# Cross attention in a two-layer decoder: latent queries by pairs of batches, as three fp32r products of 512 columns

## Chip, cores, metric

One core of a Trainium2 chip runs the whole kernel. The metric is the device time of one execution in microseconds, the median of several runs. Engines: TensorE (PE; its weight loads are shown as PEld), VectorE (DVE), ScalarE (ACT), GpSimd (POOL), and SyncE (SP), which issues the DMA transfers.

## What is computed

A decoder with two layers over x of shape (4, 256, 256) and a context of (4, 256, 64). Layer 0 is linear attention with decay, an additive cross term and a mixture of experts; layer 1 is softmax attention with rotary embedding, a cross attention with latents (the part that is changed), and another mixture of experts. A layer norm stands ahead of each part, whose output is added to x. The cross attention has 16 heads, a query latent of 192, a context latent of 64:

```python
DIM_Q, H, K, D_C, D_CQ, R = (256, 16, 128, 64, 192, 64)
# Wq (H*K, DIM_Q), w_kc_q (H, K, D_CQ), w_kc_kv (H, K, D_C)
# W_qr (H, D_CQ, R), W_kr (H, D_C, R), Wo (DIM_Q, H*K)
def _rotate_half(x):
    half = x.shape[-1] // 2
    return jnp.concatenate([-x[..., half:], x[..., :half]], axis=-1)
def _apply_rope(x, sin, cos):
    return x * cos + _rotate_half(x) * sin
```

As the kernel does it: the queries x Wq are taken into the query latent by w_kc_q, rotated, and taken by W_qr and W_kr to the 64 features of the context latent, where they meet the rotated context. Softmax over 256 context positions, the weighted context, and then w_kc_kv and Wo give the output.

## The kernel before

The program is written by hand, one instruction stream for each engine, with semaphores between them. Cross attention (`cross()` in each engine's stream) has a merging stage and a loop.

**Merging stage.** Weights arrive in four groups of four heads (`wx`, two buffers of 2 MB; the third and fourth wait until the first and second have been used). For each group TensorE computes merged queries (`merged_queries`, L1854: Wq times w_kc_q, one PSUM bank a head, banks 0 to 3), merged keys (L1867: W_qr times W_kr, banks 4 and 5) and merged outputs (L1878: w_kc_kv times Wo, bank 6). ScalarE copies the queries (L1237) and the outputs (L1230); VectorE writes the keys with a head mask in twelve 128x64 pieces a group (L836) into `merged_s`, which GpSimd has zeroed (L1330). Each group also transposes the tokens of one batch into bank 7 (L1915), and ScalarE copies them to `xT4` (L1242). After the second group TensorE computes the latent queries of the first unit, while the weights of the third are on their way. VectorE rotates the keys (L841, L843), and TensorE then transposes them (L1927).

**Loop.** There are 16 units, w = 4 batch + group, one batch of 256 tokens and one group of four heads each (L2005). A group's query latent is three tiles of 128 rows, each with two halves (`part`) for the rotation. `latent_queries(w, j)` (L1890) is one tile: two parts by two K halves, f32 128x128 by 128x256, into bank n % 2. The profile shows each f32 product as two records, so a tile is 8 records. VectorE multiplies by cosine and sine (`rope`, L820 and L821, 128x512 each), GpSimd adds the two halves into `latent_rot` (L1337, two additions of 128x256 a tile). `query_side(w)` (L1930) multiplies by `merged_s` into bank 2; ScalarE rounds the result to fp32r (`tSh`, L1266), VectorE computes the rest (`tSl`, L849), and both are wanted by `scores` (L1946, fp32r, split in three products). VectorE takes maxima (L856), ScalarE exponentials (L1252), VectorE scales (L866), TensorE transposes (L1978), ScalarE and VectorE copy (L1258, L871). `weighted_contexts` (L1982) and `output` (L1991) follow. The outputs of a batch's four units are accumulated in bank 7 and added to x once a batch (L876).

The order within a unit is written out by hand (L2005 to L2029). Latent queries of unit w+1 stand between the steps of unit w: after its query side, between the two blocks of transposes of unit w-1, and after its second scores. The output is that of unit w-2. After the loop, the expert stage of layer 1 begins, interleaved with the last unit. Its weights go through `raw` (SyncE loads, ring of five), `whi` (ScalarE) and `wlo` (VectorE): high part and rest, in fp32r, three products each (`three`, L1762).

## Time and profile before

| | us |
|---|---|
| median of 3 runs | 911.11 |
| lowest, highest | 910.43, 911.59 |
| the profiled execution | 910.82 |
| its span in the profile | 909.0 |
| TensorE busy | 887.6 (98%) |
| VectorE busy | 615.3 (68%) |
| ScalarE busy | 424.0 (47%) |
| GpSimd busy | 101.3 (11%) |

The profiled execution took 910.82 us, 1.8 more than the span of its instructions. The merging stage begins with merged queries at 414.27 us from the span's start; the loop starts at 441.13, and its last unit's scores at 672.65. TensorE's granted clock is at its full level (0.997 on average). Matmuls are pipelined, and a record lasts longer than the distance to the next one: the distance between starts is what a record costs.

### The profile page before, as it was taken

How to read it: one execution, taken by the hardware profiler on the slowest of the kernel's cores; microseconds unless marked ns; L12 is line 12 of the kernel's file. 1: busy time of each engine (PE TensorE's matmuls, PEld its weight loads, DVE VectorE, ACT ScalarE, POOL GpSimd, SP SyncE). 2: the span in 40 equal slices, each digit the busy share in tenths (PEclk: the TensorE clock that was granted, in tenths of full speed). 3: DMA queues.
4: the chain of work that ended last, by engine and by line, in shares of the span. 5: the costliest groups of instructions: out<-in, count | busy, mean ns of one | idle time of the engine just before them, and what ended most of it. 6: DMA issues, size and time to landing. Idle time of an engine off the chain costs nothing.

```text
span 909.0 us, 14200 instructions
## 1 busy us (share of the span) xinstructions
PE 887.6 (98%) x5377; PEld 687.1 (76%) x5377; DVE 615.3 (68%) x1185; ACT 424.0 (47%) x1063; POOL 101.3 (11%) x128
## 2 busy tenths in 40 slices
PE   8998999999999999999999999999999999999998
PEld 5665778888888876667877777777767778888886
DVE  4679656666666667657787786877785566666665
ACT  8554643343443479863543444344354444333342
POOL 4011000000000220003122232322210000000000
PEclk9999999999999999999999999999999999999999
DMA  6003111111100500006200000000010111111001
GB/s 189 1 7 119 36 52 53 39 48 52 35 0 1 231 1 2 1 1 265 91 2 1 1 1 1 1 1 2 0 36 18 36 53 52 53 35 52 17 0 47
DMA packets 12537, 37.10 MB, mean 41 GB/s; under 512 B 2080, under 2 KB 4352, under 8 KB 11712
## 3 DMA queue, kind: packets, MB, share of 16 engines
q1 hardware_dynamic: 12448, 36.32, 12.0%
q8 instruction: 37, 0.61, 0.3%
q14 instruction: 20, 0.16, 0.1%
q0 software_dynamic: 32, 0.01, 0.0%
HBM read 35.27 MB, written 1.05 MB: 40 GB/s over the span
## 4 chain that ended last, share of the span: by engine, by line
PE 85%; DVE 7%; ACT 5%; DMA 1%; issue 1%; POOL 0%; DVEq 0%; ACTq 0%
PE ps L1345 79%; PE ps L1978 3%; PE ps L1518 2%; DMA wx<-in_wx 1%; DVE P L542 1%; ACT Q L1134 1%; DVE stats L466 1%; ACT DT L950 1%; DVE xn L474 0%; ACT probs_q L1252 0%; ACT whi L1149 0%; DVE weighted_h L694 0%; DVE probs_q L866 0%; PE ps L1356 0%; DVE wlo L810 0%
## 5 line engine op out<-in xcount | busy, mean ns | idle before, releaser
L1179 ACT ACTIVATE h_hi<-weighted_h 128x512 fp32r<-128x512 f32 x100 | 63.2, 632 | 150.9 <-DVE weighted_h L694 148.8
L704 DVE TENSOR_TENSOR h_lo<-weighted_h,h_hi 128x512 fp32r<-128x512 f32 x100 | 69.2, 692 | 66.1 <-ACT h_hi L1179 65.9
L1345 PE MATMUL ps<-xT_first,whi 128*128 128x512 f32 x376 | 109.0, 391 | 1.2 <-ACT silu_g L1174 1.2
L1345 PE MATMUL ps<-xT_second,whi 128*128 128x512 f32 x376 | 108.5, 391 | 1.3 <-ACT silu_g L1174 1.2
L731 DVE TENSOR_TENSOR shared_gate<-silu_g,row_shares 128x512 f32<-128x512 f32 x88 | 60.9, 692 | 61.2 <-ACT silu_g L1174 61.0
L1174 ACT ACTIVATE silu_g<-ps 128x512 f32<-128x512 f32 x100 | 59.7, 598 | 73.4 <-PE ps L1345 73.4
L1345 PE MATMUL ps<-xT,merged_q 128*128 128x256 f32 x384 | 91.9, 383 | 0.0
L1337 POOL TENSOR_TENSOR latent_rot<-rope_buf 128x256 f32<-128x256 f32 x96 | 68.4, 733 | 180.4 <-DVE rope_buf L821 180.4
L1345 PEld LDWEIGHTS ps<-xT_first,whi 128*128 128x128 f32 x376 | 70.3, 188 | 17.3 <-issue 2.8
L1345 PEld LDWEIGHTS ps<-xT_second,whi 128*128 128x128 f32 x376 | 70.1, 188 | 17.0 <-issue 2.5
L1345 PEld LDWEIGHTS ps<-xT,merged_q 128*128 128x128 f32 x384 | 70.4, 190 | 10.5
L1345 PE MATMUL ps<-h_hi,wlo 128*128 128x512 f32 x200 | 78.0, 390 | 0.0
L1345 PE MATMUL ps<-h_hi,whi 128*128 128x512 f32 x188 | 74.2, 395 | 0.8 <-DVE h_lo L704 0.7
L1345 PE MATMUL ps<-h_lo,whi 128*128 128x512 f32 x188 | 73.3, 390 | 0.0
L1252 ACT ACTIVATE probs_q<-ps,neg_max 128x256 f32<-128x256 f32 x128 | 58.9, 472 | 28.7 <-DVE neg_max L856 28.7
L694 DVE TENSOR_TENSOR weighted_h<-ps,shared_gate 128x512 f32<-128x512 f32 x88 | 60.9, 692 | 8.4
L1345 PE MATMUL ps<-xT_second,wlo 128*128 128x512 f32 x200 | 61.7, 390 | 0.0
L1345 PE MATMUL ps<-xT_first,wlo 128*128 128x512 f32 x200 | 61.7, 390 | 0.0
L1134 ACT ACTIVATE Q<-ps,nm 128x256 f32<-128x256 f32 (+1 forms) x128 | 52.5, 449 | 2.4 <-DVE nm L551 2.4
L866 DVE TENSOR_SCALAR probs_q<-probs_q,rsum 128x256 f32<-128x256 f32 x128 | 49.9, 451 | 1.1
L1345 PE MATMUL ps<-latent_rot,merged_s 128*64 128x256 f32 (+1 forms) x256 | 47.4, 386 | 0.0
L1345 PEld LDWEIGHTS ps<-latent_rot,merged_s 128*64 128x64 f32 (+1 forms) x256 | 32.0, 163 | 19.3 <-issue 14.5
(197 smaller groups left out, 1572.7 us busy)
## 6 DMA issues: line engine op xcount, KB each, us to landing
raw<-in_ffn SPq DMA_DIRECT2D x50, 384.0 KB, 3.0
wx<-in_wx SPq DMA_DIRECT2D x4, 2048.0 KB, 11.2
cx<-in_cx SPq DMA_DIRECT2D x1, 1536.0 KB, 8.2
X<-in_x SPq DMA_DIRECT2D x4, 256.0 KB, 6.8
kvc<-in_kvc SPq DMA_DIRECT2D x1, 1024.0 KB, 14.3
out<-X SPq DMA_DIRECT2D x4, 256.0 KB, 2.2
wqkv<-in_wqkv SPq DMA_DIRECT2D x1, 768.0 KB, 8.2
wqkv<-in_wqkv SPq DMA_DIRECT2D x1, 512.0 KB, 6.3
```

What stands on the lines that cost most here:

```text
L694: v.tensor_tensor(weighted_h[:, u % 2, :], ps[:, 5 + u % 2, :], gate[:, u % 2, :], ALU.mult).then_inc(weighted[l], 1)
L704: v.tensor_tensor(h_lo[:, u % 2, :], weighted_h[:, u % 2, :], h_hi[:, u % 2, :].bitcast(F32), ALU.subtract).then_inc(act_lo[l], 1)
L731: v.tensor_tensor(shared_gate[:, u % 2, :], silu_g[:, u % 2, :], row_shares[:, hf, :], ALU.mult).then_inc(gated[l], 1)
L866: last = v.tensor_scalar(probs_q[:, w % 2, st, ab, pair, :], probs_q[:, w % 2, st, ab, pair, :], rsum[:, st, ab, pair:pair + 1], None, ALU ...
L1134: last = a.activation(Q[:, n % 3, i, width * h:width * h + width], step_scores(n)[:, i, width * h:width * h + width], ACT.Exp, bias=nm[:, ...
L1174: a.activation(silu_g[:, u % 2, :], ps[:, gate_bank(n), :], ACT.Silu).then_inc(silu_done[l], 1)
L1179: a.activation(h_hi[:, u % 2, :], weighted_h[:, u % 2, :], ACT.Copy).then_inc(act_hi[l], 1)
L1252: last = a.activation(probs_q[:, w % 2, st, ab, pair, :], ps[:, xscore_bank(ab), 256 * pair:256 * pair + 256], ACT.Exp, bias=neg_max[:, st ...
L1337: g.tensor_tensor(latent_rot[:, TILE_ORDER[j], part, :], r1[:, j, 256 * part:256 * part + 256], r2[:, j, 256 - 256 * part:512 - 256 * part ...
L1345: return pe.matmul(o, l, r, start=start, stop=stop, skip_group_check=True)
L1518: last = pe.transpose(ps[:, bank, 128 * c:128 * c + 128], src, ident)
L1978: last = pe.transpose(ps[:, turned_bank(ab), 256 * pair + 128 * st:256 * pair + 128 * st + 128], probs_q[:, w % 2, st, ab, pair, 128 * lt: ...
```

## The change

1. Units go by pairs of batches: w counts batch of the pair fastest, then group, then pair. A pair is what one set of latent queries serves, 512 tokens at once.
2. A latent query chunk is one tile and one part, for two batches (`latent_chunk`): 48 chunks, each three products (high weights by high tokens, low weights by high tokens, high weights by low tokens) by two K halves, in fp32r with 512 columns. So merged query weights and tokens are both split: ScalarE writes the high part, VectorE subtracts it from PSUM for the low part (`merged_ql`, second half of `xT_first` and `xT_second`). PSUM banks of the merging stage are free only after VectorE (`merged_q_low`, `xt_rest`).
3. Chunks run two units ahead instead of one: six in the merging stage (three after the second group, three after the third), three in each of the units 0 to 13, none in 14 and 15.
4. GpSimd adds pairs of chunks (128x512). The middle tile's result has two buffers. GpSimd, not VectorE, now rotates the keys, and it zeroes nothing.
5. Merged keys: one masked VectorE operation a part; the middle tile's two heads are swapped in the layout, so that a piece less is stored.
6. Each unit's output is added to x by itself (128x512), no longer accumulated over four units; batches 0 and 1 are normalised in units 10 and 11, batches 2 and 3 after the loop.
7. The expert weights of layer 1 have other places (`raw1`, `whi1`) and are loaded after the last chunk; ScalarE's first three splits of them stand in units 14 and 15.

```diff
-    for name, width in (("wq", 4 * D), ("kcq", 4 * XQ), ("qrT", 2 * 4 * LO), ("krT", 4 * XC), ("kckv", 4 * XC), ("woT", 4 * D)):
+    for name, width in (("wq", 4 * D), ("kcq", 4 * XQ), ("qrT", 2 * 4 * LO), ("krT", 6 * XC), ("kckv", 4 * XC), ("woT", 4 * D)):
...
+        def unit_batch(w):
+
+            return 2 * (w // (2 * GROUPS)) + w % 2
+
+        def unit_group(w):
+
+            return w // 2 % GROUPS
+
+        def latent_chunk(n):
+
+            pair, c = divmod(n, 6)
+            return pair, TILE_ORDER[c // 2], c % 2
...
+                if l == 1:
+                    sp.wait_ge(pe_latent, LATENT_CHUNKS)
...
+                def rope(n):
+
+                    pair, tile, part = latent_chunk(n)
                     v.wait_ge(pe_latent, n + 1)
-                    if w >= 1:
-                        v.wait_ge(latent_rotated, 2 * (n - 3) + 2)
...
+                    if n >= 3:
+                        v.wait_ge(latent_rotated, 2 * ((n - 3) // 2 + 1))
...
+                for hg in range(GROUPS):
+                    if hg % 2 == 0:
+                        merged_key_parts(hg)
+                    for jj in range(4):
+                        v.wait_ge(merged_q_copied, 4 * hg + jj + 1)
+                        v.tensor_tensor(merged_ql[:, hg, :, :, LO * jj:LO * jj + LO], ps[:, jj, 0:2 * XQ].rearrange("p (k h f) -> p k h f", k=KD, h=2),
+                                        merged_qh[:, hg, :, :, LO * jj:LO * jj + LO].bitcast(F32), ALU.subtract).then_inc(merged_q_low, 1)
+                    if hg % 2:
+                        merged_key_parts(hg)
+                    v.wait_ge(xt_ready, 8 + hg + 1)
+                    tokens, at = (xT_first, xT_second)[hg // 2], 256 * (hg % 2)
+                    v.tensor_tensor(tokens[:, 1, :, at:at + 256], ps[:, 7, :].rearrange("p (k s) -> p k s", k=KD), tokens[:, 0, :, at:at + 256].bitcast(F32),
+                                    ALU.subtract).then_inc(xt_rest, 1)
+                    if hg == 1:
+                        v.wait_ge(cx_in, 16)
+                    if hg in (1, 2):
+                        for j in range(CHUNKS_PER_UNIT):
+                            rope(CHUNKS_PER_UNIT * (hg - 1) + j)
...
+                def add_output(w):
+                    b, last = unit_batch(w), unit_group(w) == GROUPS - 1
+                    v.wait_ge(pe_xout, w + 1)
...
+            for i in range(LATENT_CHUNKS // 2):
+                pair, tile, _ = latent_chunk(2 * i)
+                g.wait_ge(rope_products, 4 * i + 4)
+                if tile == 1 and pair >= 2:
+                    g.wait_ge(pe_operand, 2 * pair - 2)
+                elif tile != 1 and pair >= 1:
+                    g.wait_ge(pe_operand, 2 * pair)
+                for part in range(2):
+                    g.tensor_tensor(rotated(pair, tile)[:, part, :], r1[:, (2 * i + part) % 3, :], r2[:, (2 * i + 1 - part) % 3, :], ALU.add).then_inc(latent_rotated, 1)
...
                     if hg >= 1:
-                        pe.wait_ge(merged_q_copied, 4 * (hg - 1) + jj + 1)
+                        pe.wait_ge(merged_q_low, 4 * (hg - 1) + jj + 1)
                     if hg == 2 and jj < 2:
                         pe.wait_ge(rope_products, 6 - 2 * jj)
+                    if hg == 3 and jj < 2:
+                        pe.wait_ge(rope_products, 10 + 2 * jj)
...
+                    for m, (weights, token_part) in enumerate(((merged_qh, 0), (merged_ql, 0), (merged_qh, 1))):
                         for kk in range(KD):
-                            last = mm(ps[:, n % 2, 256 * part:256 * part + 256], merged_q[:, hg, kk, part, 128 * tile:128 * tile + 128], xT4[:, kk, b, :], kk == 0, kk == 1)
+                            last = mm(ps[:, n % 2, :], weights[:, hg, kk, part, 128 * tile:128 * tile + 128], tokens[:, token_part, kk, :], m + kk == 0, m + kk == 3)
...
+                    if hg in (1, 2):
+
+                        pe.wait_ge(xt_rest, 2)
+                        pe.wait_ge(merged_q_low, 4 * hg + 2)
+                        for j in range(CHUNKS_PER_UNIT):
+                            latent_queries(CHUNKS_PER_UNIT * (hg - 1) + j)
+
+                pe.wait_ge(merged_q_low, 4 * GROUPS)
+                pe.wait_ge(xt_rest, NB)
                 pe.wait_ge(kv_rotated, 1)
...
                 for w in range(UNITS):
-                    more = w + 1 < UNITS
-                    if w == 1:
-                        latent_queries(2, 0)
+                    ahead = CHUNKS_PER_UNIT * (w + 2)
+                    more = ahead < LATENT_CHUNKS
                     query_side(w)
-                    if more and w != 1:
-                        latent_queries(w + 1, 0)
-                    if not more:
+                    if more:
+                        latent_queries(ahead)
+                    else:
                         output(w - 2)
                     scores(w, 0)
```

## Rows read from the trace of the kernel before

**Rows 1.** The page: busy time; TensorE's group of latent queries

```profile
PE 887.6 (98%) x5377; PEld 687.1 (76%) x5377; DVE 615.3 (68%) x1185; ACT 424.0 (47%) x1063; POOL 101.3 (11%) x128
L1345 PE MATMUL ps<-xT,merged_q 128*128 128x256 f32 x384 | 91.9, 383 | 0.0
```

**Rows 2.** Timeline of TensorE in a steady unit: start, length, what, count, [idle]

```profile
537.78 0.39 PE L1345 MATMUL ps<-kvh,tSh 64*128 64x256 f32 x2
...
538.69 1.99 PE L1345 MATMUL ps<-xT,merged_q 128*128 128x256 f32 x8
540.52 1.89 PE L1345 MATMUL ps<-merged_o,wqkv 128*128 128x256 f32 x8
...
544.10 2.96 PE L1345 MATMUL ps<-latent_rot,merged_s 128*64 128x256 f32 x16
546.90 1.89 PE L1345 MATMUL ps<-xT,merged_q 128*128 128x256 f32 x8
548.72 0.39 PE L1345 MATMUL ps<-kvh,tSh 64*128 64x256 f32 x2
```

**Rows 3.** The same timeline: first scores of units 13, 14 and 15

```profile
641.56 0.39 PE L1345 MATMUL ps<-kvh,tSh 64*128 64x256 f32 x2
...
657.17 0.38 PE L1345 MATMUL ps<-kvh,tSh 64*128 64x256 f32 x2
...
672.65 0.39 PE L1345 MATMUL ps<-kvh,tSh 64*128 64x256 f32 x2
```

**Rows 4.** The same timeline in the expert stage of layer 0

```profile
201.28 0.39 PE L1345 MATMUL ps<-h_hi,whi 128*128 128x512 f32 x1
...
202.41 0.39 PE L1345 MATMUL ps<-h_lo,whi 128*128 128x512 f32 x1
```

**Rows 5.** Timelines of ScalarE, VectorE, TensorE between query side and scores

```profile
547.10 0.60 ACT L1266 ACTIVATE tSh<-ps 128x512 fp32r<-128x512 f32 x1 [2.18 <-PE ps L1345]
...
547.73 0.69 DVE L849 TENSOR_TENSOR tSl<-ps,tSh 128x512 fp32r<-128x512 f32 x1 [2.32 <-ACT tSh L1266]
...
456.86 0.69 DVE L849 TENSOR_TENSOR tSl<-ps,tSh 128x512 fp32r<-128x512 f32 x1 [1.16 <-ACT tSh L1266]
...
457.60 0.39 PE L1345 MATMUL ps<-kvh,tSh 64*128 64x256 f32 x2 [1.41 <-DVE tSl L849]
```

**Rows 6.** Timeline of TensorE: second scores of unit 15

```profile
676.73 0.39 PE L1345 MATMUL ps<-kvh,tSh 64*128 64x256 f32 x2 [0.46 <-ACT probs_q L1252]
```

**Rows 7.** Groups of GpSimd (busy, mean ns); timelines of VectorE and GpSimd

```profile
L1337 POOL TENSOR_TENSOR latent_rot<-rope_buf 128x256 f32<-128x256 f32 x96 | 68.4, 733 | 180.4 <-DVE rope_buf L821 180.4
L1327 POOL TENSOR_TENSOR P<-P 128x512 f32<-128x512 f32 x8 | 10.2, 1273 | 230.1 <-DVE P L490 230.1
...
540.21 1.14 DVE L866 TENSOR_SCALAR probs_q<-probs_q,rsum 128x256 f32<-128x256 f32 x4
...
542.67 2.09 DVE L866 TENSOR_SCALAR probs_q<-probs_q,rsum 128x256 f32<-128x256 f32 x4
...
542.63 1.46 POOL L1337 TENSOR_TENSOR latent_rot<-rope_buf 128x256 f32<-128x256 f32 x2 [2.83 <-DVE rope_buf L821]
```

**Rows 8.** The chain that ended last; merging stage: TensorE's timeline, ScalarE's copies (min/median/max)

```profile
646.02 0.60 DVE rope_buf L821
...
417.07 11.86 DMA wx<-in_wx
...
417.72 5.38 PE L1345 MATMUL ps<-wx 128*128 128x192 f32 x36 [0.24 <-ACT merged_q L1237]
...
423.53 5.34 PE L1345 MATMUL ps<-xT,merged_q 128*128 128x256 f32 x24
...
428.97 5.41 PE L1345 MATMUL ps<-wx 64*128 64x128 f32 x36
...
441.13 3.01 PE L1345 MATMUL ps<-latent_rot,merged_s 128*64 128x256 f32 x16
...
L1237 ACT ACTIVATE merged_q<-ps x16: 482/491/548, 417.1 to 437.5; 128x384 f32<-128x384 f32 x16
```

More of the change, by code:

```diff
@@ L347, in build, with rotated, output_added @@
         UNITS = NB * GROUPS
+        CHUNKS_PER_UNIT = 3
+        LATENT_CHUNKS = CHUNKS_PER_UNIT * UNITS
         TILE_ORDER = (1, 0, 2)
+        def unit_batch(w):
[5 more added lines that the diff above has]
+            return pair, TILE_ORDER[c // 2], c % 2
+        def rotated(pair, tile):
+            return middle_rot[:, pair % 2] if tile == 1 else outer_rot[:, tile // 2]
+        def output_added(w):
+            if unit_group(w) < GROUPS - 1:
+                return x_added, (2 * GROUPS - 2) * (w // (2 * GROUPS)) + w % (2 * GROUPS) + 1
+            return x_done, 8 * 4 + 2 * unit_batch(w) + 2
         def xscore_bank(ab):
@@ L881, in cross @@
                 for w in range(UNITS):
-                    more = w + 1 < UNITS
+                    ahead = CHUNKS_PER_UNIT * (w + 2)
+                    more = ahead < LATENT_CHUNKS
                     operand_rest(w)
+                    if not more and w >= 2:
+                        add_output(w - 2)
                     if more:
-                        rope(w + 1, 0)
-                    else:
+                        rope(ahead)
+                    elif w == UNITS - 1:
                         split_lo(1, 0, 0)
@@ L891, in cross @@
                     if more:
-                        rope(w + 1, 1)
-                    else:
+                        rope(ahead + 1)
+                    elif w == UNITS - 1:
                         split_lo(1, 1, 1)
@@ L896, in cross @@
                         copy_transposed(w - 1, 1)
-                    if w == 0:
-                        rope(1, 2)
                     row_max(w, 1)
                     normalise_probs(w, 0)
-                    if more and w >= 1:
-                        rope(w + 1, 2)
+                    if more:
+                        rope(ahead + 2)
                     normalise_probs(w, 1)
-                    if w % GROUPS == 1 and w > 1:
-                        add_output(w // GROUPS - 1)
-                    if w % GROUPS == 2 and w > 2:
-                        normalise(5, w // GROUPS - 1)
+                    if more and w >= 2:
+                        add_output(w - 2)
+                    if w in (2 * GROUPS + 2, 2 * GROUPS + 3):
+                        normalise(5, w - 2 * GROUPS - 2)
                 tokens_low(1, 0)
+                add_output(UNITS - 2)
                 copy_transposed(UNITS - 1, 0)
@@ L1930, in query_side @@
                 def query_side(w):
-                    pe.wait_ge(latent_rotated, 6 * w + 2)
+                    pair_of_batches, columns = w // 2, slice(256 * (w % 2), 256 * (w % 2) + 256)
+                    pe.wait_ge(latent_rotated, 6 * pair_of_batches + 2)
                     if w >= 1:
                         pe.wait_ge(operand_lo, w)
-                    group = w % GROUPS
+                    group = unit_group(w)
                     for part in range(2):
@@ L1938, in query_side @@
                             half = slice(64 * (1 - pair), 64 * (1 - pair) + 64)
-                            mm(ps[half, 2, 256 * pair:256 * pair + 256], merged_s[:, group, part, 1 + pair, half], latent_rot[:, 1, part, :], part == 0, False)
+                            mm(ps[half, 2, 256 * pair:256 * pair + 256], merged_s[:, group, part, 1, half], rotated(pair_of_batches, 1)[:, part, columns], part == 0, False)
                     for pair in range(2):
-                        pe.wait_ge(latent_rotated, 6 * w + 4 + 2 * pair)
+                        pe.wait_ge(latent_rotated, 6 * pair_of_batches + 4 + 2 * pair)
                         for part in range(2):
-                            last = mm(ps[:, 2, 256 * pair:256 * pair + 256], merged_s[:, group, part, 3 * pair, :], latent_rot[:, 2 * pair, part, :], False, part == 1)
+                            last = mm(ps[:, 2, 256 * pair:256 * pair + 256], merged_s[:, group, part, 2 * pair, :], rotated(pair_of_batches, 2 * pair)[:, part, columns], False, part == 1)
                     last.then_inc(pe_operand, 1)
                 def scores(w, st):
-                    b = w // GROUPS
+                    b = unit_batch(w)
                     if w == 0 and st == 0:
@@ L2017, in cross @@
                     if more:
-                        latent_queries(w + 1, 1)
+                        latent_queries(ahead + 1)
                     if w >= 1:
                         transposed_probabilities(w - 1, 1)
-                    if w == 0:
-                        latent_queries(1, 2)
                     scores(w, 1)
-                    if more and w >= 1:
-                        latent_queries(w + 1, 2)
+                    if more:
+                        latent_queries(ahead + 2)
                     if w >= 2 and more:
@@ L2070, in constants @@
     head = (np.arange(3)[None] * P + p[:, None]) // LO
-    put("gmask", head[:, :, None] == np.arange(3)[None, :, None] + np.arange(2)[None, None, :])
+    put("gmask", head[:, :, None] == np.array(TILE_HEADS)[None])
     put("even", (p // HD) % 2 == 0)
@@ L2125, in cross_pack @@
     put("qrT", by_group(i["L1_xattn_W_qr"].reshape(XH, 2, LO, XR), 0, 4, 2, 1, 3))
-    put("krT", by_group(i["L1_xattn_W_kr"], 0, 3, 1, 2))
+    put("krT", by_group(i["L1_xattn_W_kr"], 0, 3, 1, 2)[:, :, [h for pair in TILE_HEADS for h in pair]])
     put("kckv", by_group(i["L1_xattn_w_kc_kv"], 0, 2, 1, 3))
```

176 lines of the change are left out of this document (84 added, 92 removed).

## The prediction

> **What bounds the kernel now.** I read the page first: TensorE is busy for 98% of the span, and its largest group inside cross attention is the latent queries, 384 records of 128x256 f32 [rows 1]. Then one unit of cross attention (of 16) in TensorE's timeline. Call S0 and S1 the two score blocks of a unit, L a block of latent queries, T transposed probabilities, O the output, W weighted contexts, Q the query side of the next unit. The order is S0, T, L, T, S1, L, O, W, Q, L. S0 starts at 548.72 and at 641.56: six units, 15.47 us each, with no idle bracket on TensorE [rows 2, 3]. So in the steady units anything that leaves TensorE's queue is worth its time, until the chain through ScalarE, VectorE and GpSimd that feeds it is late. So the question of the whole reading is where those chains end.
>
> **Records of latent queries.** An L of 8 f32 records takes 1.82 us (546.90 to 548.72) [rows 2], 0.2275 a record. An fp32r product with 512 columns is one record; five in a row in the expert stage start 0.226 apart (201.28 to 202.41) [rows 4]. A record thus costs the same and only the count matters. Before: 48 blocks x 8 = 384. After: 48 chunks x 6 = 288 (three products x two K halves, for two batches at once). Removed: 96 x 0.2275 = 21.8 us of TensorE work. A chunk takes 6 x 0.227 = 1.36 us in place of 1.82.
>
> **Steady units (2 to 12).** Taking three times 0.455 out of 15.47 leaves 14.10. Three chains could be late.
> (a) Between Q and S0: ScalarE rounds the operand 0.20 after L starts (547.10 against 546.90), VectorE's rest starts 0.63 later (547.73) [rows 2, 5]. Where it is exposed, the rest runs from 456.86, 0.69 long, and S0 starts at 457.60 [rows 5]. So S0 cannot start sooner than 0.20+0.63+0.69+0.05 = 1.57 after L. L used to cover this with 1.82; at 1.36 it no longer does: 0.21 of stall per unit.
> (b) S0 to S1 waits for four exponentials. In the last unit, where nothing covers them, it is 676.73-672.65 = 4.08, ended by ScalarE [rows 3, 6]. In a steady unit it is 15.47-(548.72-537.78) = 4.53 [rows 2], and 0.455 less is 4.08: just covered.
> (c) Rotation by GpSimd. It now adds pairs of chunks, 128x512 each; such an addition takes 1.27, a 128x256 one 0.73 [rows 7]. So it works in bursts of 2.55 us, and in odd units the last burst begins after the third rotation product. VectorE's work from S0 is: two products (0.6 each [rows 8]) to 1.15, two maxima to 2.4, a copy to 3.0, two products to 4.5 (waiting for L), copy to 5.1, maxima to 6.4, scaling to 7.6, products to 8.85. The burst ends at 11.45. S1 lasts 0.91 and O and W 3.58 together (540.52 to 544.10), so Q starts at 4.08+0.91+1.36+3.58 = 9.95 and reaches the products that need it after two thirds of its 2.80 us [rows 2], at 11.8. Margin 0.35 us, so no stall, but little room.
> The new addition of each unit's output (128x512, 0.6 on VectorE, in place of two smaller ones every fourth unit) falls at 11 to 12.6, before the operand rest at 13.6, hidden; without that cover it would be 0.6 a unit. O waits only for the addition of a unit earlier.
> A steady unit is 14.10+0.21 = 14.31, a gain of 1.16; eleven of them: **-12.8 us**. Bounds: 14.10 (chain (a) shorter than it looks) to 14.9 (0.3 at (b), 0.6 at (c) in every other unit), -15 to -6.
>
> A row bears on (c): scaling four 128x256 tiles takes 1.14 alone, but 2.09 when it starts at 542.67 beside a GpSimd burst that starts at 542.63 [rows 7]. Bursts now last 2.55, so VectorE could lose about 1.9 there in an odd unit rather than 0.95; that ends at 12.0, still before 13.6, and is not in the sum. The Trainium skill (SBUF — State Buffer, "Who interferes with whom") says that the two engines lock a shared port pair for a whole instruction and that the loser fully blocks. By that rule the longer instructions block VectorE longer, which speaks against this change. The trace agrees as to the direction (2.09 against 1.14), and by either reading the loss lies in VectorE's slack.
>
> **Merging stage: what is added.** All of the first pair's chunks (6, not 3 blocks) now stand here: 6x1.36 - 5.34 [rows 8] (at 423.53) = +2.8 us of work. The rest is new waiting, since a PSUM bank comes free only after VectorE has subtracted, behind ScalarE's copy (0.49) [rows 8]. VectorE's 128x384 subtraction is not in this trace; 0.46 is scaled from 0.60 for 512, bounds 0.2 and 0.6. Step by step:
> - The second group's merged queries start at 417.72 now [rows 8]. VectorE first has the merged keys (2 x 0.46 where twelve small ones stood) and then four subtractions from 418.4, first done 418.9: **1.2** late. The whole group then ends at 424.5 with its transposes.
> - The first chunk needs the second batch's tokens too: merged-output copy, token copy, subtraction (0.5+0.5+0.6): it starts at 426.0, not 423.53, **1.5** of it idle.
> - Three chunks end at 430.15. The weights that ended the wait at 428.93 [rows 8] are 3% larger and should have landed; that wait goes, and what is late next is TensorE itself.
> - Third group and transposes, 5.6: chunks 3 to 5 run 435.75 to 439.95. The rotation of chunk 5 reuses a buffer of chunk 2, which GpSimd reads from 438.55 (after chunk 3's products) to 441.1. Its products end at 442.4, and the fourth group's second head waits for that bank: **1.8** idle. GpSimd itself has the rotation of the keys first (three 1024-wide operations, an estimate of 2.4 each at twice 1.27, from 424 to 431.2); the first pair is rotated by 433.8, in time.
> - Fourth group to 447.3; then the last tokens' copy and subtraction (**1.4**), key transposes, and the loop starts at 449.4 instead of 441.13.
> Sum: **+8.3 us**. Bounds: +2.8 if no new wait shows, +10 if subtractions take 0.6 and each hand-over 0.1 more.
>
> **First and last units.** From loop start to the second unit's S0: 457.60-441.13 = 16.47 now [rows 5, 8]. After: Q 2.80, 1.57, S0 to S1 3.9 (no copy ahead of the exponentials), 0.91, 1.36, 2.80, 1.57 = 14.91: **-1.6**. Unit 1 has no O, so Q starts at 8.2 and its last products would be due at 10.05, before the GpSimd burst ends at 11.45: 13.95 against 641.56-11x15.473-457.60 = 13.76: **+0.2**. Unit 13: two L go, the last L becomes an O of the same length, 657.17-641.56 = 15.61 less 0.91, plus small change: **-1.05**. Unit 14 has no latent queries left, so it is bound by the exponentials as unit 15 is: 4.08, S1 0.91, W 1.76, Q 2.80 and O 1.82 = 11.4 against 672.65-657.17 = 15.48 [rows 3]: **-4.1**. At the end, an addition (0.6 [rows 8]), statistics (an estimate of 0.7, two reads of 256 columns) and the normalisation of the third batch move into the tail beside other work; in unit 15 two additions come before its maxima: **+0.4** (bounds 0 and 2).
>
> Moved transfers: the expert weights' first five loads wait for the last chunk, near 640, and are needed near 658; such a load lay well under that apart, so nothing. Both queues' other work keeps its place.
>
> **Sum.** +8.3-1.6+0.2-12.8-1.05-4.1+0.4 = -10.65. The profiled execution took 910.82 (span 909.0, 1.8 around it): 900.2 after, with a span of 898.4. The median of the runs is 0.3 above the profiled one: 900.5.
>
> **Rivals.**
> 1. *New waits don't bite.* If the merging stage costs only its +2.8 of work plus some 1.5, and (a) is covered, the sum is +4.3-1.6-15.1-1.05-4.1+0.4 = -17: about 894. For: VectorE has slack in that stage; against: the ring TensorE, ScalarE, VectorE is traced step by step above. 15%.
> 2. *The GpSimd burst is late in odd units.* Margin is 0.35. If the third rotation products slip by 1 us (blocked scaling, other order), six odd units lose 0.65, (b) loses 0.2 in eleven: +6, about 906.5. 15%.
> 3. *Slower: changing between f32 and fp32r.* At a change of type the first record may cost more. If entry and exit each cost 0.2 us, 48 chunks lose 19 us, and the result is about 920. It decides from 10.6/48 = 0.22 a chunk. Against it: the score blocks are fp32r between f32 blocks already and no gap stands at 548.72 [rows 2]. 4%.
> 4. *Gains and costs cancel:* waits of rival 2 in every unit and the upper bound in the merging stage, near 911. 3%.
>
> **How the numbers follow.** The forecast, 897 to 904 around 900.5, has 63%, the rivals 15, 15, 4 and 3. The range 892.5 to 908 takes in rivals 1 and 2 and leaves out 3 and 4 and the ends of the bounds. 0.2% (1.8 us) is about what a measurement here can tell from no change. Faster 0.93, same 0.03, slower 0.04.
>
> **What the profile after would show.** 288 latent-query records of 128x512, 0.227 apart; S0 14.3 us apart in the steady units, with a 0.2 idle bracket before it released by VectorE's operand rest; some 35 us from the first group to the loop start with idle brackets before the second group, the first chunk, the fourth group's second head and the key transposes; an S0 distance of 11.4 in unit 14. The prediction is wrong if the loop starts before 446 or after 452, if TensorE waits for GpSimd in odd units, or if a chunk takes over 1.5 us.

## The result, and the profile after

| | us |
|---|---|
| after, median of 5 runs | 906.5 (905.9 to 907.8) |
| before, median of 5 runs beside it | 910.89 |
| ratio after/before, 95% interval | 0.9954 (0.9942 to 0.9965) |
| the profiled execution after, and its span | 906.39, 904.6 |

The change is faster by 4.4 us, beyond the 0.2% that can be told from no change; the forecast was a gain of 10.65. The page of after: TensorE is busy for 13.6 us less than in [rows 1], but the span is only 4.4 shorter, so some 9 us of idle time were added. GpSimd has fewer instructions (79 for 128) and is busy for 3 us less.

```profile
PE 874.0 (97%) x5281; PEld 666.8 (74%) x5281; DVE 628.5 (69%) x1170; ACT 421.4 (47%) x1063; POOL 98.1 (11%) x79
```

The gain does not lie where the time was added, so the first thing to make is a ledger by stage, from the starts in TensorE's timeline of either kernel:

| stage | before | after | moved | forecast |
|---|---|---|---|---|
| start to the first merged queries | 414.27 | 414.51 | +0.24 | 0 |
| merging stage, to the loop's start | 26.86 | 36.98 | +10.12 | +8.3 |
| loop's start to S0 of unit 1 | 16.47 | 15.26 | -1.21 | -1.6 |
| unit 1 | 13.75 | 14.23 | +0.48 | +0.2 |
| units 2 to 12 | 170.21 | 160.11 | -10.10 | -12.8 |
| unit 13 | 15.61 | 14.98 | -0.63 | -1.05 |
| unit 14 | 15.48 | 11.35 | -4.13 | -4.1 |
| S0 of unit 15 to the end | 236.35 | 237.18 | +0.83 | +0.4 |
| sum | | | -4.40 | -10.65 |

Two terms carry most of the miss of 6.25: the steady units (2.7) and the merging stage (1.8). The other six add 1.7.

**A steady unit after.** TensorE's timeline from S1 of one unit to S0 of the next (start, length, what, count, [idle]):

```profile
484.22 1.03 PE L2043 MATMUL ps<-cst,probs_q 128*128 128x128 f32 x8
485.18 0.39 PE L1405 MATMUL ps<-kvh,tSh 64*128 64x256 f32 x2
...
486.09 0.73 PE L1405 MATMUL ps<-xT_first,merged_qh 128*128 128x512 f32 x2
...
487.57 1.89 PE L1405 MATMUL ps<-merged_o,wqkv 128*128 128x256 f32 x8
...
491.16 1.03 PE L1405 MATMUL ps<-middle_rot,merged_s 128*64 128x256 f32 x8
...
493.77 0.82 PE L1405 MATMUL ps<-xT_first,merged_qh 128*128 128x512 f32 x2
...
495.53 0.39 PE L1405 MATMUL ps<-kvh,tSh 64*128 64x256 f32 x2
```

The chunk behind S1 lasts 487.57-486.09 = 1.48. The block that it replaces lasted 540.52-538.69 = 1.83 [rows 2], so 0.35 is saved and not the 0.455 of the forecast. Transposes and the block behind them went from 2.65 to 2.33, 0.32 less.

The block behind Q has to be read together with Q. From Q's start to S0 it was 548.72-544.10 = 4.62 and is 495.53-491.16 = 4.37, exactly the forecast's 2.80+1.57. Q looks 0.19 shorter (2.61 for 2.80) and the chunk behind it 0.19 longer than forecast (1.76 for 1.57), but that is one thing counted twice: the chunk's first record starts earlier beside Q's last ones. ScalarE, which needs the finished Q, starts 2.99 behind Q's start, 3.00 before. The whole unit: 0.32+0.35+0.25 = 0.92, and the period went from 15.47 to 14.55.

Does chain (a) hold S0 up? TensorE's timeline shows no idle bracket, because a matmul record ends later than the next one may start. The lines of ScalarE and VectorE, and the chunk's last record:

```profile
494.15 0.60 ACT L1317 ACTIVATE tSh<-ps 128x512 fp32r<-128x512 f32 x1 [2.18 <-PE ps L1405]
494.79 0.69 DVE L894 TENSOR_TENSOR tSl<-ps,tSh 128x512 fp32r<-128x512 f32 x1 [2.44 <-ACT tSh L1317]
495.12 0.39 PE L1405 MATMUL ps<-xT_first,merged_qh 128*128 128x512 f32 x1
```

S0 starts at 495.53, 0.05 behind the end of the operand rest (494.79+0.69), as where it was exposed before (457.60, [rows 5]). So chain (a) does end last. Its size: S0 stands 0.41 behind the chunk's last record. Before, where the operand rest ended 0.30 ahead of S0 (548.72 against 547.73+0.69), that distance was 0.31 (548.72-548.41). So the wait is 0.10 a unit, not the 0.21 of the forecast; the longer chunk fills the rest. The weight loads say about the same:

```profile
495.53 0.19 PEld L1405 LDWEIGHTS ps<-kvh,tSh 64*128 64x128 f32 x2 [0.46 <-DVE tSl L894]
548.72 0.19 PEld L1345 LDWEIGHTS ps<-kvh,tSh 64*128 64x128 f32 x2 [0.33 <-DVE tSl L849]
```

The first line is after's and the second before's. A bracket of 0.33 that names VectorE stands there even where nothing is late, so only the 0.13 above it count.

**Why 0.35 and not 0.455.** Three answers of TensorE's timeline of before, with windows that begin inside a block, give its single records; under them, after's records of one chunk:

```profile
538.69 0.48 PE L1345 MATMUL ps<-xT,merged_q 128*128 128x256 f32 x1
539.01 0.59 PE L1345 MATMUL ps<-xT,merged_q 128*128 128x256 f32 x2
539.22 1.46 PE L1345 MATMUL ps<-xT,merged_q 128*128 128x256 f32 x6
```

```profile
486.43 0.39 PE L1405 MATMUL ps<-xT_first,merged_qh 128*128 128x512 f32 x1
```

Before, the second record starts 0.32 after the first (539.01-538.69) and the other starts are (540.52-539.01)/7 = 0.216 apart. After, the second starts 0.34 after the first (486.43-486.09) and the others are (487.57-486.43)/5 = 0.229 apart. So the f32 record of 256 columns is cheaper than the fp32r record of 512, and a block has some 0.1 beside its records: behind the scores at its entry (as here), ahead of the scores at its exit (the 0.31 above). Before's block between two blocks of transposes has none of it, 552.28-550.55 = 1.73 for eight records:

```profile
550.55 1.89 PE L1345 MATMUL ps<-xT,merged_q 128*128 128x256 f32 x8
552.28 1.04 PE L1978 MATMUL ps<-cst,probs_q 128*128 128x128 f32 x8
```

The prediction divided the 1.82 of the block ahead of the scores by 8, which spread that 0.1 over the records and gave 0.2275. Eight records at 0.216 less six at 0.229 to 0.232 are 0.33 to 0.35, and 48 chunks save about 16.6 us, not 21.8.

**The merging stage after.** TensorE's timeline, with the brackets to look for:

```profile
414.51 2.76 PE L1405 MATMUL ps<-wx 128*128 128x192 f32 x16
...
419.25 5.38 PE L1405 MATMUL ps<-wx 128*128 128x192 f32 x36 [1.55 <-DVE merged_ql L876]
...
426.63 0.74 PE L1405 MATMUL ps<-xT_first,merged_qh 128*128 128x512 f32 x2 [1.41 <-DVE xT_first L882]
...
444.10 4.73 PE L1405 MATMUL ps<-wx 128*128 128x192 f32 x32 [1.76 <-DVE rope_buf L861]
...
450.88 0.68 PE L1991 MATMUL ps<-cst,wqkv 64*128 64x64 f32 x8 [1.46 <-issue]
451.49 1.08 PE L1405 MATMUL ps<-middle_rot,merged_s 128*64 128x256 f32 x8
```

The four waits stand where the forecast had put them (1.2, 1.5, 1.8, 1.4) and measure 1.55, 1.41, 1.76 and 1.46. The last one's bracket names no releaser; VectorE's subtraction of the last tokens ends at 450.78, 0.10 ahead of the key transposes, as the forecast had it.

### The profile page after: what moved, and what is told of

The parts are those of the page before. It is cut to its first block, busy times and chain, and to the rows that moved or that the text cites. A ratio compares the mean times of both kernels' runs of the same rounds, so it can differ in the third digit from the quotient of the medians.

```text
span 904.6 us, 13933 instructions
## 1 busy us (share of the span) xinstructions
PE 874.0 (97%) x5281; PEld 666.8 (74%) x5281; DVE 628.5 (69%) x1170; ACT 421.4 (47%) x1063; POOL 98.1 (11%) x79
## 3 DMA queue, kind: packets, MB, share of 16 engines
HBM read 35.54 MB, written 1.05 MB: 40 GB/s over the span
## 4 chain that ended last, share of the span: by engine, by line
PE 82%; DVE 9%; ACT 6%; issue 2%; POOL 1%; DVEq 0%; ACTq 0%; POOLq 0%
PE ps L1405 76%; PE ps L2043 3%; PE ps L1578 2%; DVE P L580 1%; ACT Q L1184 1%; ACT probs_q L1303 1%; POOL outer_rot L1398 1%; DVE stats L504 1%; DVE rope_buf L861 1%; DVE xn L512 1%; ACT DT L1000 1%; ACT whi L1199 0%; DVE wlo L848 0%; DVE weighted_h L732 0%; DVE neg_max L901 0%
## 5 line engine op out<-in xcount | busy, mean ns | idle before, releaser
L861 DVE TENSOR_TENSOR rope_buf<-ps,cx 128x512 f32<-128x512 f32 x96 | 61.7, 684 | 9.4 <-PE ps L1405 6.9
L911 DVE TENSOR_SCALAR probs_q<-probs_q,rsum 128x256 f32<-128x256 f32 x128 | 54.5, 488 | 1.1
L1398 POOL TENSOR_TENSOR outer_rot<-rope_buf 128x512 f32<-128x512 f32 x32 | 41.4, 1313 | 100.4 <-DVE rope_buf L861 100.4
L589 DVE TENSOR_REDUCE nm<-ps 128x4 f32<-128x1024 f32 (+1 forms) x24 | 29.2, 1219 | 24.6 <-PE ps L1405 24.6
L848 DVE TENSOR_TENSOR wlo<-raw,whi 128x768 fp32r<-128x768 f32 x47 | 45.0, 957 | 1.9
L1405 PEld LDWEIGHTS ps<-xT_second,wlo 128*128 128x128 f32 x200 | 37.5, 188 | 8.0
## 6 DMA issues: line engine op xcount, KB each, us to landing
kvc<-in_kvc SPq DMA_DIRECT2D x1, 1024.0 KB, 14.6
```

The source lines that it names most:

```text
L848: v.tensor_tensor(wlo[:, slot, :], (raw0, raw1)[l][:, slot, :], high_weights(l, c // RING if isinstance(c, int) else c, slot)[:, slot, :]. ...
L861: v.tensor_tensor(r[:, n % 3, :].rearrange("p (b s) -> p b s", b=2), x, kx(table)[:, at:at + 256].unsqueeze(1).to_broadcast([P, 2, SEQ]), ...
L911: last = v.tensor_scalar(probs_q[:, w % 2, st, ab, pair, :], probs_q[:, w % 2, st, ab, pair, :], rsum[:, st, ab, pair:pair + 1], None, ALU ...
L1398: g.tensor_tensor(rotated(pair, tile)[:, part, :], r1[:, (2 * i + part) % 3, :], r2[:, (2 * i + 1 - part) % 3, :], ALU.add).then_inc(laten ...
L1405: return pe.matmul(o, l, r, start=start, stop=stop, skip_group_check=True)
```

## The experiments

All comparisons are with the kernel before, run beside them on the same chip (910.45 in the first group, 910.74 and 910.7 in the others); after is 906.5, measured beside 910.89.

**1. Four products in place of three** (`e2_four_products`): eight records a chunk.

```diff
-  for m, (weights, token_part) in enumerate(((merged_qh, 0), (merged_ql, 0), (merged_qh, 1))):
+  for m, (weights, token_part) in enumerate(((merged_qh, 0), (merged_ql, 0), (merged_qh, 1), (merged_ql, 1))):
```

> Changed kernel with a fourth product in each chunk (low weights by low tokens), 8 records for 6. Theory A: blocks two and three of a unit cost 0.45 more each, the one after the query side 0.25 (its own 1.56 grows to 2.01, where 1.76 is spent now), 1.16 x 14 = 16, and up to 2.7 in the merging stage: 922 to 925. Rival B: 96 x 0.227 = 21.8 more, about 928.3. Theory A above all expects that taking two records away (the other run) gives half of what adding two costs; B expects the same of both.

Measured: 926.18 (925.29 to 927.23), ratio 1.017 (1.0153 to 1.0187). S0 goes from 486.22 to 502.07 without an idle bracket, a period of 15.85, 1.30 above after's 14.55. The chunks behind T and S1 grew by 0.46 to 0.47 for two records and the one behind Q by 0.38, because it had 0.1 of wait in it. So a record costs 0.23 on the path, and the 0.1 beside the records is not paid again. The time is 1.2 above the first theory's range and 2.1 below the rival's. The period grew by 0.14 more than expected (11 units, 1.5 us), and the clock, too, took a part: behind the wait ahead of the key transposes the granted clock is 0.50 from 454 to 456, and the eight records of `outer_rot` take 3.32 where after's take 1.99.

```profile
452.30 0.68 PE L1991 MATMUL ps<-cst,wqkv 64*128 64x64 f32 x8 [1.46 <-issue]
...
454.23 3.32 PE L1405 MATMUL ps<-outer_rot,merged_s 128*128 128x256 f32 x8
```

**2. Two products in place of three** (`e1_two_products`): the product of the high weights with the low tokens is left out, and with it one of the two correction terms.

```diff
-  for m, (weights, token_part) in enumerate(((merged_qh, 0), (merged_ql, 0), (merged_qh, 1))):
+  for m, (weights, token_part) in enumerate(((merged_qh, 0), (merged_ql, 0))):
```

> Changed kernel with one of the three products of each latent-query chunk left out (high weights by low tokens), so 4 records a chunk for 6; its output lacks that term. Theory A (a block costs an entry of about 0.11 us and 0.227 a record; the block between query side and scores is covered by the chain ScalarE to VectorE, and the block between the first and second scores by the exponentials): the first block gives nothing, the second 0.12, the third 0.45 a unit, 0.57 x 14 = 8, and some 1.5 in the merging stage: about 897. Rival B (TensorE's records are all on the path): 96 x 0.227 = 21.8 less, about 884.7.

Measured: 902.09 (901.15 to 902.38), ratio 0.9906 (0.9889 to 0.9922). Both numbers are missed, the first theory's by 5. Its steady unit nearly holds (14.05 on average over units 2 to 12, 13.98 expected), and the timeline shows why taking away records is worth so little there, waits ahead of S0 and of S1:

```profile
552.27 0.39 PE L1405 MATMUL ps<-kvh,tSh 64*128 64x256 f32 x2 [0.48 <-DVE tSl L894]
556.34 0.39 PE L1405 MATMUL ps<-kvh,tSh 64*128 64x256 f32 x2 [0.27 <-ACT probs_q L1303]
566.36 0.39 PE L1405 MATMUL ps<-kvh,tSh 64*128 64x256 f32 x2 [0.48 <-DVE tSl L894]
```

But the merging stage lasts 451.74-414.20 = 37.54, where after's lasts 36.98 and its shorter chunks should have made it shorter. The busy time by stretches (length; busy time of PE, PEld, DVE, ACT, POOL with counts; granted clock, DMA share, GB/s) shows it in the column of the clock:

```profile
442.00:444.00 2.00, 1.33 (x5) 1.36 (x6) 0.99 (x2) 0.00 (x0) 1.40 (x2) 0.71 0.03 8
444.00:446.00 2.00, 2.00 (x8) 2.00 (x7) 0.61 (x2) 0.98 (x2) 1.16 (x1) 0.50 0.00 0
...
452.00:454.00 2.00, 2.00 (x12) 1.34 (x9) 1.67 (x2) 0.00 (x0) 0.00 (x0) 0.77 0.00 0
454.00:456.00 2.00, 2.00 (x7) 1.57 (x5) 0.00 (x0) 0.00 (x0) 0.00 (x0) 0.50 0.00 0
```

Twice the granted clock falls to 0.50, the lower of its two levels (1.2 GHz), for some 3 us. TensorE's timeline of the same stretch has what stood before it and what was slow behind it:

```profile
442.67 6.41 PE L1405 MATMUL ps<-wx 128*128 128x192 f32 x32 [1.95 <-DVE rope_buf L861]
...
451.13 0.68 PE L1991 MATMUL ps<-cst,wqkv 64*128 64x64 f32 x8 [1.46 <-issue]
...
452.75 3.48 PE L1405 MATMUL ps<-outer_rot,merged_s 128*128 128x256 f32 x8
```

TensorE had been idle for 1.95 and for 1.46. The 32 records of merged queries last 6.41 where after's last 4.73, and the eight of `outer_rot` 3.48 where after's last 1.99. That is 1.7 in the merging stage and 1.5 in the loop's first Q, 3.2 us together and most of the 5 by which the first theory missed. Without the 1.7 the stage would be 1.1 shorter than after's, not by the 2.7 of its twelve records fewer: in each half the third chunk now waits for its bank (0.52 and 0.73, VectorE's rotation). After had idle stretches of 1.76 and 1.46 at the same places and kept its clock at 1.00.

**3. f32 products of 512 columns** (`e3_f32_chunks`): the pairing and all the rest of the change, but one f32 product of the rounded high parts in place of the three fp32r ones (both low parts are left out of the product, though still computed).

```diff
-  for m, (weights, token_part) in enumerate(((merged_qh, 0), (merged_ql, 0), (merged_qh, 1))):
-      for kk in range(KD):
-          last = mm(ps[:, n % 2, :], weights[:, hg, kk, part, 128 * tile:128 * tile + 128], tokens[:, token_part, kk, :], m + kk == 0, m + kk == 3)
+  for kk in range(KD):
+      last = mm(ps[:, n % 2, :], merged_qh[:, hg, kk, part, 128 * tile:128 * tile + 128].bitcast(F32), tokens[:, 0, kk, :].bitcast(F32), kk == 0, kk == 1)
```

> Changed kernel with each chunk as f32 products of 512 columns (two, one a K half) in place of six in fp32r; the operands are the rounded high parts and the low parts are left out, though VectorE still writes them. It separates the pairing of batches from the split. If an f32 record costs by its columns (0.2157 at 256, so 0.43 at 512), a chunk is 0.11 + 4 x 0.43 = 1.83 against 1.47: 0.36 more in two blocks of a unit and 0.1 in the covered one, 0.82 x 14 = 11.5, and about 2 in the merging stage: about 920, so pairing alone costs 9 against the kernel before, and the split brings 13.5. Rival: the pairing itself (fewer, longer instructions, fewer entries) brings part of the gain, and the time stays under 911.

Measured: 919.11 (918.87 to 919.24), ratio 1.0094 (1.0077 to 1.0111), as expected. This splits the change: pairing, splitting and the new merging stage cost 8.7 us by themselves, and fp32r products in place of f32 ones give back 12.6.

**4. Output between query side and scores** (`e4_output_after_query`). From unit 2, O takes the place of the chunk between Q and S0, and the unit's three chunks stand between the scores: Q, O, S0, T, L, L, T, L, S1, W.

```diff
                     query_side(w)
-                    if more:
+                    if w < 2:
                         latent_queries(ahead)
                     else:
                         output(w - 2)
                     scores(w, 0)
...
+                    if w >= 2 and more:
+                        latent_queries(ahead)
                     if more:
                         latent_queries(ahead + 1)
```

> Changed kernel, from the third unit on the output of unit w-2 stands between the query side and the scores in place of a latent chunk, and the three chunks stand between the two scores. Theory A: the 1.57 us of ScalarE and VectorE are covered by the output's 1.82, nothing waits, and a unit is 14.34 for 14.55: 12 x 0.21 = 2.5 less, 904. Rival: the wait isn't what the block costs, and it only moves (to GpSimd's additions before an even unit's query side, or to VectorE): 906.5 or more.

Measured: 904.21 (903.64 to 905.78), ratio 0.9936 (0.992 to 0.9953), as expected. The period falls from 14.55 to 14.28, with one unit of 14.9 (609.85 to 624.77). The bracket of the loads ahead of S0 falls from 0.46 to between 0.33 and 0.35, the size that it has where nothing waits: O, 1.82 long, covers chain (a), which the chunk did not. But the wait was only 0.10 to 0.13, so less than half of the 0.27 comes from it, and the number agrees partly by luck. The order also has fewer changes of block; TensorE's timeline shows a block of 12 records in one piece:

```profile
540.14 0.72 PE L1407 MATMUL ps<-xT_second,merged_qh 128*128 128x512 f32 x2
...
543.02 1.03 PE L2045 MATMUL ps<-cst,probs_q 128*128 128x128 f32 x8
```

12 records in 2.88, where two blocks of six take 1.49+1.48 = 2.97: one entry less, 0.09 saved. What is left of the 0.27, some 0.05 to 0.08, is not taken apart.

**5. The merging stage's order** (`e5_last_group`, `e6_all_groups`). In the fourth group the token transposes go first, then keys and outputs, then the queries, and of these the heads whose banks wait for the rotation (0 and 1) go last (`head_order` gives 3, 2, 0, 1). In the second kernel the first two groups are treated alike: tokens ahead of keys and outputs, and VectorE subtracts low queries and low tokens ahead of the key parts.

```diff
-                for jj in range(4):
+                for jj in head_order(hg):
...
+                    if hg == 3:
+                        turned_batch(hg)
-                    if hg == 2:
+                    if hg >= 2:
                         merged_keys(hg)
                         merged_outputs(hg)
                     merged_queries(hg)
```

> From the changed kernel, the order within the fourth group of the merging stage: its token transposes stand first, then the merged keys and outputs, then the four heads' queries with the two outer heads last swapped to the front (3, 2, 0, 1). The key transposes wait for one low part fewer. The arithmetic is the same. Theory A (the stage lost more than forecast by waits of its order: 1.76 before the fourth group's second head and 1.46 before the key transposes in the changed kernel's trace): both waits go, the loop starts 3 to 3.8 us earlier, nothing else changes: 903. Theory B (the stage is paced by its inputs, the weights' DMA and GpSimd's rotation, and the waits only move): the loop starts within 0.5 us of 451.5, 906 or more.

> The fourth group as in the run before, and in groups 0 to 2 the token transposes first too, with VectorE subtracting the low tokens and low queries ahead of the key parts in groups 0 and 1. Theory A: the waits of 1.55 and 1.41 at the start of the stage of the changed kernel shrink as well, which gives 0.5 to 2 us more: 901 to 902.5. Theory B (the early waits are waits for the weights' transfer, which the order does not touch): the same time as the run before within 0.5 us.

Measured: 903.61 (902.98 to 904.7), ratio 0.9921 (0.9905 to 0.9938), and 901.02 (900.22 to 901.41), ratio 0.989 (0.9874 to 0.9907). Both as the first theory had it. The merging stage lasts 449.10-415.62 = 33.48 in the first and 446.30-415.12 = 31.18 in the second, where after's lasts 36.98. In both runs the stage began later than in after, by 1.1 and 0.6, ahead of anything that was changed, and so the time fell by less than the stage. TensorE's timeline of the second:

```profile
419.22 2.84 PE L1421 MATMUL ps<-wx 128*128 128x192 f32 x16 [0.91 <-DVE merged_ql L888]
421.90 0.60 PE L1987 MATMUL ps<-cst,xn 128*128 128x128 f32 x4
422.43 2.62 PE L1421 MATMUL ps<-wx 64*128 64x128 f32 x20
424.97 0.73 PE L1421 MATMUL ps<-xT_first,merged_qh 128*128 128x512 f32 x2
...
439.79 0.60 PE L1987 MATMUL ps<-cst,xn 128*128 128x128 f32 x4
440.32 5.41 PE L1421 MATMUL ps<-wx 64*128 64x128 f32 x36
445.67 0.71 PE L2014 MATMUL ps<-cst,wqkv 64*128 64x64 f32 x8
446.30 1.08 PE L1421 MATMUL ps<-middle_rot,merged_s 128*64 128x256 f32 x8
```

Three of the four waits are gone and the first is 0.91. They came from the order of the steps, not from the weights' transfer.

**6. Both** (`e7_groups_and_output`): the reordered merging stage and O between Q and S0.

> The run before with the output block between the latent query block and the scores from unit 2 on. Theory A (the two gains lie in different stretches and add up; the loop's order alone gave 906.4 to 904.2): 898.5 to 900. Theory B (an earlier loop start meets the same data later, or the stage's gain is given back at the loop's start): 902 or more.

Measured: 897.78 (897.29 to 898.05), ratio 0.9856 (0.9839 to 0.9872). The gains add up, and a little more: 5.5 and 2.3 alone, 8.7 together. This is the fastest kernel that computes everything, 13 us below before, three times what the change itself gave.

**7. Two products again, on that order** (`e8_two_products_reordered`); the edit of experiment 2 on the kernel of experiment 6, with the same term left out.

> The last kernel (merging stage reordered, output between query side and scores) with the product by the low tokens left out: four records a chunk in place of six (the latent queries' smallest term is missing). Alone, on the changed kernel's order, this cut gave 4.3 us of the 21.8 that 96 records take; its trace showed waits on both sides of the scores and TensorE's granted clock at half (0.50) for some 2 us at 444 and 2 at 454, behind idle stretches of the merging stage. Theory A (what stood in the way there is the order: the operand's and the exponentials' chains were exposed, and the idle stretches that preceded the low clock are gone in this order): a steady unit falls from 14.28 by nearly 6 x 0.227 = 1.36 to 12.9-13.1, the merging stage loses 1.5 to 2.7, no stretch at half clock in 440 to 460: 880 to 886. Theory B (VectorE, GpSimd and ScalarE bound a unit whatever the order): the period stays above 13.7, and it ends at 891 to 895.

Measured: 886.58 (886.18 to 890.77), ratio 0.9747 (0.9721 to 0.9773), 11.2 below the kernel of experiment 6, where the same cut on after's order gave 4.4. The granted clock stays at 1.00 from 412 to 462, as the first theory had it. The merging stage itself gives only 1.0 (30.18 for 31.19) and not the 1.5 to 2.7 expected: each half's third chunk waits for its bank (0.52 and 0.74), and the third group for its weights:

```profile
429.15 5.41 PE L1423 MATMUL ps<-wx 64*128 64x128 f32 x36 [0.47 <-DMA wx<-in_wx]
```

Most of the gain comes from the loop (units 2 to 12: 147.7 for 157.6). S1 goes from 506.57 to 519.45 (12.88, as the first theory had it) and then to 533.21 (13.76). The time is 0.6 above that theory's range; the short gain of the merging stage and every second unit are the reasons:

```profile
523.09 1.13 PE L1423 MATMUL ps<-outer_rot,merged_s 128*128 128x256 f32 x4
524.80 1.13 PE L1423 MATMUL ps<-outer_rot,merged_s 128*128 128x256 f32 x4 [0.58 <-POOL outer_rot L1416]
```

```profile
518.20 2.59 POOL L1416 TENSOR_TENSOR outer_rot<-rope_buf 128x512 f32<-128x512 f32 x2 [9.12 <-DVE rope_buf L865]
522.26 2.49 POOL L1416 TENSOR_TENSOR outer_rot<-rope_buf 128x512 f32<-128x512 f32 x2 [1.47 <-DVE rope_buf L865]
```

GpSimd's second burst, begun at 522.26 and over at 524.75, now ends last. So the price of 0.23 a record is real as long as neither the chains around S nor the burst is exposed; the change's own order had chain (a) exposed by 0.1, and the burst is next: from unit 2 on every second unit takes 13.8 or more.

**8. Three chunks in one block** (`e9_joined_chunks`), on the kernel of experiment 6.

```diff
-                    if w >= 1:
-                        transposed_probabilities(w - 1, 1)
                     if w >= 2 and more:
                         latent_queries(ahead + 2)
+                    if w >= 1:
+                        transposed_probabilities(w - 1, 1)
                     scores(w, 1)
```

> The last kernel (merging stage reordered, output between query side and scores) with the third chunk of a unit ahead of the second block of transposes, so that all three chunks stand behind one another: 18 records in one block, not 12 and 6. The same arithmetic. Theory A (each block of latent queries pays some 0.11 at its entry, its second record starting 0.34 behind the first where the others are 0.227 apart): 12 units with one entry less, the 18 records from first start to the next block's start 4.2 to 4.25, the period 14.28 less 0.1 = 14.18, 896.5. Theory B (no cost at the entry, the 0.34 is the drain of the block before or only how the start is recorded): the same time as the last kernel within 0.3 us, 897.5 to 898. A loss beyond that would be a wait for the third chunk's bank.

Measured: 902.03 (901.96 to 902.74), ratio 0.9904 (0.9888 to 0.9921), 4.2 above the kernel of experiment 6: neither theory, but the loss that the expectation names behind them, and one more. TensorE's timeline and its weight loads:

```profile
549.90 0.72 PE L1423 MATMUL ps<-xT_second,merged_qh 128*128 128x512 f32 x2
...
554.43 1.03 PE L2068 MATMUL ps<-cst,probs_q 128*128 128x128 f32 x8
555.39 0.39 PE L1423 MATMUL ps<-kvh,tSh 64*128 64x256 f32 x2
```

```profile
552.93 0.30 PEld L1423 LDWEIGHTS ps<-xT_second,merged_qh 128*128 128x128 f32 x2 [0.42 <-DVE rope_buf L865]
...
560.06 0.73 PEld L1423 LDWEIGHTS ps<-outer_rot,merged_s 128*128 128x128 f32 x4 [0.27 <-POOL outer_rot L1416]
```

The 18 records take 4.53 in this unit and 4.61 in the next, where twelve and six take 2.89+1.55 = 4.44 in the kernel of experiment 6. The entry between them is gone, but the third chunk waits some 0.3 for its bank (VectorE's rotation of the first). The transposes ahead of S1 last 0.96, where ahead of a chunk they last 0.79 in the kernel of experiment 6; but a chunk's first record starts earlier beside the block ahead of it and its second comes later (0.32), so 0.08 of these 0.17 is only another way of counting. And Q is longer in every second unit (2.95 for 2.79), because its products wait for GpSimd's burst. The period became 14.6 to 14.7, 0.3 to 0.4 above 14.28. So what a block costs beside its records depends on its neighbours, and joining two blocks gives nothing when a bank or a burst is then waited for.

## Why the prediction was half right

The direction was right, and the order of the stages too: the merging stage pays, the steady units and unit 14 gain. The size was 2.4 times too large.

- **Records of latent queries: the step that failed.** "A record thus costs the same and only the count matters", 96 x 0.2275 = 21.8. By the records' distances it is about 16.6. The f32 record is 0.216 and the fp32r record 0.23, and the 0.2275 was a block's length over its count, with some 0.1 in it that belongs to the switch to the scores. The near match of 0.2275 with the expert stage's 0.226 [rows 4] made it look confirmed. Per chunk 0.35 went, not 0.455; experiment 1 measured the record on the path. This step alone accounts for about 3.7 of the 6.25: 2.6 in the steady units, 0.2 in unit 13, 0.6 in units 0 and 1 (where the chunk behind S1 lasts 1.58) and 0.3 in the merging stage.
- **Steady units.** 14.31 was forecast, 14.55 measured; 11 x 0.24 = 2.7, which is the step above in two chunks of a unit (0.13 and 0.11) and nothing else.
- **Chain (a)** was right in its mechanism and in its end: S0 comes 4.37 behind Q's start, as forecast, 0.05 behind the operand rest. The stall is 0.10 and not 0.21, because the chunk that stands in front of it is longer than forecast; in the unit's sum the two cancel.
- **Chain (b) and the bursts (c)** were forecast as hidden and are: from unit 2 to 12 TensorE waits for neither (S0 to S1 is 4.20, where 4.08 was the chain's own length). GpSimd's additions last 1.31 and the burst 2.56 to 2.60, as expected. Rival 2's wait stands in unit 1 alone, where the forecast had it too (1.40 from its working, 1.13 measured); with fewer records it comes in every other unit (experiment 7).
- **VectorE beside the burst.** Four scalings took 3.24 beside GpSimd, 1.14 alone:

```profile
647.73 1.14 DVE L911 TENSOR_SCALAR probs_q<-probs_q,rsum 128x256 f32<-128x256 f32 x4
...
650.19 3.24 DVE L911 TENSOR_SCALAR probs_q<-probs_q,rsum 128x256 f32<-128x256 f32 x4
```

  The GpSimd burst beside the second line runs from 650.15 to 652.75. The loss is 2.1, near the 1.9 of the forecast, and it stays in VectorE's slack. That two engines lock a shared port pair is what the Trainium skill says (SBUF — State Buffer, "Who interferes with whom"); the trace agrees, 3.24 against 1.14.
- **Merging stage.** Forecast +8.3, bound +10, measured +10.12. The four waits were each right within 0.35 and sum to 6.2 where 5.9 stood, although VectorE's subtraction lasts 0.55 alone and not 0.46. The miss of 1.8 lies in three places. From the stage's start to the first chunk it is 0.4, mostly the first wait. The two halves of chunks last 4.71 and 4.52 where 4.15 and 4.20 stood, 0.9 more: the third chunk of each half waits for its rotation, 0.33 and 0.26 (its groups of four records last 1.42 and 1.35, the ones before them 1.09), and the rest is the records' price. From the fourth group to the loop it is 10.03 where 9.45 stood, 0.6 more, spread over the hand-overs. Neither the waits of the third chunks nor that 0.6 were in the sum.
- **Unit 14** is exact (11.35 against 11.4). Unit 13, the loop's start and the tail missed by 0.4 each and all in one direction. More than half of it is the chunks' price in the first two; the rest, and the tail, no experiment took apart.
- **Rival 3**, a cost of changing between f32 and fp32r, is not what happened. The 0.1 beside the records stands before the change as well, and also between blocks of one type: O, with f32 blocks on either side, took 542.34-540.52 = 1.82 for its eight records.
- **The range** of 892.5 to 908 was opened upwards for rival 2, whose price was about 906.5. That the time is the same is luck: rival 2's wait for GpSimd occurs in unit 1 alone.
- **The signs.** The loop starts at 451.49, inside the 446 to 452 that was named, and a chunk takes 1.48 in a steady unit, just under the 1.5 that would have spoken against the prediction (1.76 behind Q, with the wait in it). So neither sign catches the step that failed. The 0.2 bracket ahead of S0 doesn't show in TensorE's timeline; the wait is read from the operand rest and the weight loads.

## What to carry to other kernels

Don't divide a block's time by its records when the change alters their number. Take the distance of two records inside a block and what stands beside them at each neighbour as separate prices. When TensorE's work shrinks, ask first which work covers each chain: here moving one block (O ahead of the scores) and reordering one stage gave 8.7 us, more than the change. And look at the clock column of the stretches behind a wait: here low clock cost about as much again as the wait itself.

## What the runs showed of the chip

- Consecutive f32 records of 256 columns start 0.216 apart, fp32r records of 512 columns 0.229 to 0.232 apart.
- A block of matmuls can cost some 0.1 beside its records, by its neighbours: behind the scores the second record of a latent-query block starts 0.32 (f32) or 0.34 (fp32r) after the first; ahead of the scores the distance from its last record is 0.31 to 0.32; between two blocks of transposes the f32 block had none of it (1.73 for eight). Why is open; no run here isolates it.
- The granted clock fell to 0.50 for some 3 us behind idle stretches of 1.95 and 1.46 (experiment 2) and of 1.46 (experiment 1, where 1.17 before it had no such effect), and not behind 1.76 and 1.46 in after. So the length of the idle stretch doesn't settle it. It cost 1.3 to 1.7 us each time. No run here takes this apart further.
